# When a scan stage does the next layer's projections: packed into consecutive steps instead of spread out

## The reference

```python
x = x + L0_attn(_layernorm(x))                     # selective scan, both directions
x = x + L0_xattn(ctx_1024, _layernorm(x))          # latent cross-attention
x = x + L0_ffn(...)                                # and nine more sublayers

# L0_attn, for each direction: u = silu(conv(x @ W_in)), 512 channels, state of 16
delta = softplus(dt @ Wdt + bdt)
dA, dBu = exp(delta * A), delta * B * u
h = dA * h + dBu;  y = sum_n(h * C) + u * D        # a scan over 256 positions
# out = ((y_fwd + y_bwd) / 2 * silu(z)) @ W_out

# L0_xattn: x and the context (8, 77, 256) are layer-normed twice, then
q, k, v = x @ Wq, [x; ctx] @ Wk, [x; ctx] @ Wv     # 16 heads of 64
```

## Time and profile before

| | us |
|---|---|
| three runs | 4060.97, 4080.15, 4078.96; median 4078.96 |
| the profiled execution | 4060.97, its span 4059.2 |
| scan stage, first to last scan | 70.7 to 1034.9 |
| share of the whole span: PE, DVE, ACT, POOL | 91%, 75%, 56%, 33% |
| mean granted TensorE clock | 0.958 of full speed |

### The profile page before, as it was taken

The page is one execution under the profiler, slowest core; times in us unless marked ns, Lnnn a source line. Parts: engine busy times, 40 slices in busy tenths (PEclk is TensorE's granted clock), DMA queues, the critical chain, the costliest instruction groups (busy, mean ns, idle before and its releaser), DMA issues. The chain is left out here.

```text
span 4059.2 us, 57651 instructions
## 1 busy us (share of the span) xinstructions
PE 3684.8 (91%) x20026; PEld 2563.8 (63%) x20026; DVE 3032.4 (75%) x7078; ACT 2287.5 (56%) x5545; POOL 1358.8 (33%) x873
## 2 busy tenths in 40 slices
PE   5888988989899989999999998888898889889998
PEld 2334334344566778997888896555565568645787
DVE  6899989999787767667788776677576774455777
ACT  5676776776565532224555558577677642243446
POOL 3989888999100000001233323465311200010000
PEclk8998999999899999999999998799999999999999
DMA  3554545667531000000000001000000000100000
GB/s 126 152 160 154 171 159 169 190 183 236 180 88 44 28 27 30 22 11 15 1 1 1 1 1 44 15 1 1 13 2 20 1 24 1 43 0 21 1 1 22
DMA packets 144152, 239.57 MB, mean 59 GB/s; under 512 B 23303, under 2 KB 66831, under 8 KB 141175
## 3 DMA queue, kind: packets, MB, share of 16 engines
q1 hardware_dynamic: 113187, 211.96, 16.6%
q10 hardware_dynamic: 30676, 23.93, 1.8%
HBM read 209.29 MB, written 26.54 MB: 58 GB/s over the span
## 5 line engine op out<-in xcount | busy, mean ns | idle before, releaser
L1279 DVE TENSOR_TENSOR_SCAN db<-PS,db 128x512 f32<-128x512 f32 x512 | 591.6, 1205 | 54.8 <-ACT PS L1244 36.7
L209 PE MATMUL PS<-db,cst 128*128 128x512 f32 x1024 | 494.9, 623 | 22.7 <-DVE db L1284 21.4
L216 PE MATMUL PS<-cst,p 128*128 128x128 f32 (+1 forms) x2880 | 394.1, 282 | 47.7 <-DVE pt L3510 16.7
L2250 POOL TENSOR_TENSOR rb<-rb,tb 128x512 f32<-128x512 f32 x32 | 42.9, 1343 | 1097.4 <-DVE tb L2245 1097.4
L216 PEld LDWEIGHTS PS<-cst,p 128*128 128x128 f32 (+1 forms) x2880 | 329.3, 147 | 121.1 <-issue 57.0
L209 PEld LDWEIGHTS PS<-db,cst 128*128 128x128 f32 x1024 | 200.9, 200 | 282.1 <-issue 234.4
L209 PE MATMUL PS<-xnT,W 128*128 128x256 f32 (+2 forms) x880 | 326.2, 513 | 50.6 <-ACT gate L1085 15.9
L1225 POOL TENSOR_TENSOR db<-du,b 128x1024 f32<-128x1024 f32 x128 | 303.9, 2397 | 40.1 <-PE PS L209 39.2
L1225 POOL TENSOR_TENSOR db<-W,b 128x1024 f32<-128x1024 f32 x128 | 309.8, 2447 | 12.2 <-PE PS L209 11.8
L209 PEld LDWEIGHTS PS<-xnT,W 128*128 128x128 f32 (+1 forms) x880 | 168.2, 197 | 181.6 <-issue 115.1
L2101 ACT ACTIVATE W<-PS,W 128x512 f32<-128x512 f32 x144 | 98.8, 689 | 288.5 <-PE PS L209 270.3
(11 more groups left out here) (467 smaller groups left out, 8451.3 us busy)
## 6 DMA issues: line engine op xcount, KB each, us to landing
b<-bc_rows SPq DMA_DIRECT2D x256, 256.0 KB, 3.7
c<-bc_rows SPq DMA_DIRECT2D x256, 256.0 KB, 4.0
qk<-fore_qk SPq DMA_DIRECT2D x48, 294.5 KB, 2.9
fore_qk<-W ACTq DMA_DIRECT2D x48, 256.0 KB, 3.1
W<-in_we SPq DMA_DIRECT2D x9, 1024.0 KB, 4.8
W<-in_w SPq DMA_DIRECT2D x48, 128.0 KB, 3.8
fore_v<-W ACTq DMA_DIRECT2D x24, 256.0 KB, 3.1
v<-fore_v SPq DMA_DIRECT2D x6, 1024.0 KB
```

The source lines that it names most:

```text
L209: ins = T.matmul(out, l, r, start=first and i == 0, stop=last and i == len(pairs) - 1)
L216: ins = T.transpose(bank[0:m, c:c + r], s, ident[0:r, 0:r])
L1279: V.tensor_tensor_scan(db[:, f, r], self.ring.PS[:, self.BANKS[x % 3], r], db[:, f, r], 0.0, ALU.mult, ALU.add).then_inc(self.sc.sem, 1)
L2250: e.eng.tensor_tensor(self.rb[t % 2], self.rb[t % 2], self.tb[t % len(self.tb)], ALU.add).then_inc(self.rg.sem, 1)
```

## The change

`Fore` had a span of steps for each group and spread the outputs evenly over the free ones. Now it has a start and a least distance for each group, and takes the first free steps from there (distance 2 for the context, 1 for the chunks). Free steps are counted otherwise: the steps just after y changes are no longer left out, all steps with `GATE` or `OUT` are, and from step 224 on every step is free. The output product of a chunk moves from steps 71 to 74 (`ADDX` 72 to 75) of 64 to steps 75, 77, 79, 81 (76, 78, 80, 82), so that each of its banks is held for two steps. The norm of chunk 2 starts at 211 and not at 204. The steps that come out:

| outputs | before | after |
|---|---|---|
| context | 7 8 10 12 14 15 17 20 24 26 30 37 43 46 54 56 58 59 61 63 76 77 79 81 84 86 90 94 | 7 9 11 13 15 17 28 30 32 34 37 40 43 46 49 54 56 58 60 62 66 71 73 76 78 80 82 92 |
| chunk 0 | 104 107 110 113 118 120-124 126 127 139-141 143-146 148 152 154 156 158 | 104 107 110 113 118-127 130 135-138 140 142 144 146 156 |
| chunk 1 | 168 171 174 177 182-191 203-210 212 214 | 168 171 174 177 182-191 194 199-202 204 206 208 210 219 |
| chunk 2 | 218-220 222 223 225 229 230 232 233 235 236 238-240 242 243 245-247 249 250 252 253 | 222-245 |

```diff
             for j in range(5) if c < 3 else ():
-                self.todo[64 * c + 71 + j].append((self.OUT, c, j))
-                self.todo[64 * c + 72 + j].append((self.ADDX, c, j))
+                self.todo[64 * c + 75 + 2 * j].append((self.OUT, c, j))
+                self.todo[64 * c + 76 + 2 * j].append((self.ADDX, c, j))
         self.inn.late = {1: 1, 2: 49, 3: 113}
-        self.nxt.early, self.nxt.brisk = {0: 83, 1: 147, 2: 204}, (2,)
+        self.nxt.early, self.nxt.brisk = {0: 83, 1: 147, 2: 211}, (2,)
...
-    @classmethod
-    def on_pe(cls, what, k, j):
-
-        return j % 2 == 0 if what == cls.GATE else what == cls.OUT and j < 4 or what == cls.READY and j in cls.ON_PE
...
-    CHUNKS, SPANS, LATEST, GAIN = 3, ((7, 101), (102, 165), (166, 217), (217, 255)), 6, 4
+    CHUNKS, START, APART, LATEST, GAIN = 3, (7, 102, 166, 222), (2, 1, 1, 1), 6, 4
...
-        free = [i for i in range(len(todo)) if (i - 2) % 32 > 2 and not any(Mamba.on_pe(*x) for x in todo[i])]
+        free = [i for i in range(len(todo)) if i >= 224 or not any(
+            x[0] in (Mamba.GATE, Mamba.OUT) or x[0] == Mamba.READY and x[2] in Mamba.ON_PE for x in todo[i])]
...
-        for i, (lo, hi) in enumerate(self.SPANS):
-            k, at = self.early if i == 0 else 24, [x for x in free if lo <= x < hi]
-            self.steps += [at[j * len(at) // k] for j in range(k)]
+        for i, s in enumerate(self.START):
+            steps = []
+            for x in free:
+                if x >= (steps[-1] + self.APART[i] if steps else s):
+                    steps.append(x)
+            self.steps += steps[:self.early if i == 0 else 24]
```

## The result

| | before | after |
|---|---|---|
| median of ten runs each, us | 4077.64 (4059.8 to 4081.8) | 4097.87 (4083.6 to 4118.9) |
| profiled execution, span | 4060.97, 4059.2 | 4095.32, 4093.5 |
| scan stage, first scan to the end of the last unit | 966.6 | 1004.05 |
| span behind the stage | 3021.9 | 3018.7 |
| mean granted TensorE clock | 0.958 | 0.955 |

The ratio is 1.0066, with a 95% interval of 1.0043 to 1.0090: the loss is real, and small. The stage, however, is 37.5 us longer in the profiled execution, where the working had summed to 14.2. So the total lay near the forecast, and the sum behind it was far too small.

What follows compares the result with a forecast made beforehand. Taken as bound: the scan stage, with VectorE, TensorE and GpSimd near their limit in its last 120 us. Terms 3.8 + 1.7 + 3.0 + 3.0 + 2.0 + 1.7 - 1.0 = +14.2 us; from median 4078.96, 4093 us, range 4064 to 4108.

Steps and rivals of the forecast that it cites:

- The copies in ScalarE's stretches: Abs-to-Identity stretches bound by ScalarE: net seven more copies of 0.54 us, +3.8 us, bounds 0 and 5.9.
- Additions to X: Twelve additions move to steps 76 to 82 of each chunk: 5.0 us, waits absorb 3.3, leaving +1.7, bounds 0 and 5.0.
- The norm: Chunk 2's norm seven steps later: scaling behind the Silu 2.06 us, second Sqrt 1.2 more; net +3.0, bounds 1 and 4.
- Gating y in step 226: Five groups, not three, in steps 222 to 226: VectorE waits for TensorE, +3.0 us, bounds 1.7 and 4.
- Steps 228 to 245: Three-step cycles need 10.4 us of TensorE against 9.37 of VectorE; six cycles overrun by 2 us, bounds 0 and 6.
- the reserve of 5.0 us: In steps 228 to 245, how far TensorE may fall back; the new y's first group takes about 3 of it.
- Steps 194, 66 and 130: A group ahead of the sums for gating: +1.7 us at 194; 0 at 66 and 130, upper bound 1.7 each.
- Relief: Steps 8 to 14: groups spread by twos no longer wait for the previous group's bank; -1 us, bounds 0 and -3.
- The banks: Rival: TensorE stands about 1.8 us at twelve places for output-product banks, 21 us on top, 4114 us; chance 0.18.
- the wait behind the Silu: Sign: the wait before the scan of step 220 would be near 5 us and not 2.96.
- the scans' waits: Sign: the forecast would be wrong if scans' waits for ScalarE and GpSimd together stayed under 60 us.
- bonus: At the end, the last twelve sums might take 5.3 us if the clock is up; counted 0, bound -2.9 us.

Runs made afterwards that it cites:

- the changed kernel's three relatives: Three kernels, each the changed kernel with one difference: k5_no34, k6_158, and one where GpSimd waits in step 74 for VectorE's max-and-add; stages 995.9 to 997.4 us.
- k2_tail_norm: Kernel before with chunk 2's groups at 222 to 245 and its norm at 211; stage 979.0 us against 966.6, total of one run 4085.8.
- k4_gap: Changed kernel without groups in steps 226 to 228, chunk 2's list running on to 248; stage 995.3 us against 1004.05.
- k6_158: Changed kernel with the group of step 130 moved to 158; step 162 took 6.15 us against 9.07, stage within 995.9 to 997.4.
- k5_no34: Changed kernel with the group of step 34 moved to 24; step 34 took 7.46 us against 8.41, stage within 995.9 to 997.4.
- k1_tail: Also called the tail kernel: kernel before with only chunk 2's groups moved to 222 to 245; stage 976.1 us against 966.6, total of one run 4072.6.
- k9_outport: Kernel before with chunks 0 and 1's output product and additions moved, GpSimd held in steps 74 and 138 for VectorE's max-and-add; stage 975.6 us against 966.6.
- k3_out: Kernel before with only the output product and additions of chunks 0 and 1 at their new steps; stage 979.9 us against 966.6.

## Why the prediction came near, and where it was wrong

*The copies in ScalarE's stretches* (+3.8). The mechanism was right where the stretches are free of other trouble. Steps 72 to 76 went from 20.88 to 21.62 us in the changed kernel's three relatives, with two copies more (1.1 forecast); 136 to 140 from 20.87 to 22.81, and 200 to 204 from 21.40 to 22.81, with three each (1.6 forecast). With the output product moved and GpSimd held, but the lists as before, the first two stayed at 20.88, so it is the copies.

*Additions to X* (+1.7). With the port and the banks apart, chunk 0 showed +0.6 us in 75 to 90. No run separates the last chunk. The stretch of steps 195 to 218 is 5.3 us longer, of which the norm is 0.3 and the copies some 1.4 to 1.6; the remaining 3.5 us are shared between additions, groups and the late products, and that stays open.

*The norm* (+3.0). The part behind the Silu was right: 1.96 us against 2.06. The part of the second Sqrt was too large: step 217 went from 2.32 to 2.59 us, 0.3 against 1.2, so more of it was covered than the working had allowed. What the step left out is that the late norm also delays the groups that need it: 2.5 us in step 226, which are a part of the next term (the earlier trace rows show the room of 0.47 us). The norm alone cost 4.9 us.

*Gating y in step 226* (+3.0). The count of eleven terms was right, and the mechanism. The size was 5.95, beyond even the upper bound of 4: the terms were priced at full clock and with a start as before. The low clock adds 1.8 us and the late start 1.0. `k2_tail_norm`, with the same five groups and the same late start at full clock, took 9.04 us in this step and not 10.72. This is a mis-sized term.

*Steps 228 to 245* (+2.0, up to 6). Measured +5.7. The overrun per cycle was forecast at 1.0 us and was 0.83 to 0.92. What was too large is the estimate of what is left of the reserve of 5.0 us: the pause behind the gating took 2.64 us and the slow matmuls after it 1.8, not 3 in all, and TensorE came to 226 already late. So nearly every cycle paid. Without the wait for that bank, in `k4_gap`, five cycles passed free of loss.

*Steps 194, 66 and 130.* +1.72 us against 1.7 at 194, and in this execution 0.2 at 66 and nothing at 130. At 66 that was luck: +1.9 and +3.0 us in `k6_158` and `k5_no34`, the latter beyond the bound of 1.7, by slow matmuls.

*Relief* (-1.0). Steps 8 to 19 gave 1.8 us, 1.0 of which also came in the tail kernel, where the code was as before. The stall of step 123 became 2.9 us shorter, where the working had said that it stays.

*The banks* were a rival with 0.18, excluded from the sum with the reason that buffers were free long before GpSimd came. That reason failed in its general form: 3.1 us in steps 82 to 90 of this execution (0.6 in two relatives), 4.6 in 139 to 149, and 8.4 in `k9_outport`. It is far below the rival's price of 21 us.

*Missed altogether.* Step 34 and what follows (+6.7 us): I compared the lists for groups in the steps in which y is gated, and wrote down 66, 130, 194 and 226, but not the first. The port (step 74: +4.7 us in this execution, +1.0 where VectorE was served first; over steps 72 to 76, which hold the two copies as well, +3.0 and +0.7). Step 162 (+2.9, in the changed kernel and two of its relatives).

*What cancelled.* The stage came to +37.5 us in this execution, and to about +29 to +31 in the relatives, not to +14.2. The profiled executions are 34.4 us apart and the medians 20.2: the profiled execution of before lies 17 us below the median of its ten, that of after 3 us. Whether the slower executions lose this in the stage or behind it, no trace shows. I had added the sum to the median; with a sum of 29 to 37 us the same recipe would have said 4108 to 4116 us, above what was measured. So the direction and the mechanisms that had been named hold, but that 4093 came within 5 us is luck in good part: a sum that was too small met medians that lie closer together than the stages do. The ratio gives +27 us (18 to 37), nearly twice the sum.

Of the signs that I had named: the wait behind the Silu came (5 us), the wait before the gating was 5.85 and not near 3, GpSimd was released by TensorE in the last stretch, the scans' waits rose to 65.2 (over 60), and no bonus came at the end. The five steps from 72 took 23.8 us and not 21.9, by the port; in the relatives they took 21.6.

## What to carry to other kernels

A list of optional work that runs beside a recurrence is worth checking at each point where the main chain reads a sum: list all such points by their formula (here every 32nd step), and put nothing ahead of the sum in the step itself, and little in the steps before it. When a producer is moved later, follow its first consumer: what follows a pause of TensorE may run at the low clock, and is worth pricing at both. And when one execution is compared with medians, compare stage with stage first, since an unchanged remainder of the program moved here by up to 20 us.

## What the runs showed of the hardware

VectorE's 128x1024 max-and-add with two SBUF inputs took 1.2 to 3.3 us as a rule, and 6.1 to 6.7 us where GpSimd's three products ran through beside it; with GpSimd held, 1.5 to 1.9. The Trainium skill (SBUF — State Buffer, SBUF: two separate sides) says that such an operation and GpSimd share a port pair that one of them holds for a whole instruction, while the other is blocked. The trace agrees for one instruction. It shows besides that the one that waits isn't always served at the border between two instructions: VectorE waited through the rest of three products in a row in five places (two of `k3_out`, one each of `k1_tail`, `k4_gap` and the changed kernel), and was served behind the first in `k5_no34` and `k6_158`. What decides between these is open.

TensorE's granted clock was 0.82 in the first 2 us behind the pause of 3.25 us in step 222, then 0.57, and 1.00 from 956.7 on; values between 0.50 and 1.00 are means over a stretch that has both levels. Behind the pause of 2.64 us it was 0.50, the lower of the two levels, for 3.4 us. The matmuls behind the pause of 1.68 us in `k4_gap` kept their full rate. These longer pauses (2.64, 3.01 and 3.25 us) cost another 1.8 to 2.9 us after their end. But the length of a pause alone doesn't tell: behind the same 3.56 us ahead of step 66 the granted clock was 1.00 in one execution and 0.50 in another, and `k1_tail` has two pauses of 2.26 us near the end, with twelve matmuls in 7.11 us behind one and in 5.56 behind the other. What decides is open.
